# Two adaLN layers on one core: own tiles for the last batch's second layer, and a new order table

## The chip, the core and the metric

The kernel runs on one core of one Trainium2 chip. The metric is the device time of one execution in microseconds (us); a comparison uses the median of several executions. Engines: TensorE (PE) for matrix products, VectorE (DVE), ScalarE (ACT) and GpSimd (POOL) for the rest, SyncE (SP) for issuing transfers. Each engine works off its own list of instructions in order, and waits on semaphores for the others.

## The reference

Eight batches of 512 tokens of width 128 pass through two layers. `adaln` stands for layer norm times (1 + c) plus s, with s and c from a small product of the batch's conditioning row; `g` is a gate row of the same product.

```python
# layer 0, per batch
h = layernorm(x) * (1 + ca) + sa
q, k, v = split(h @ w_qkv.T, heads=16)      # head width 8
q, k = rope(q), rope(k)
x = x + ga * (softmax(q @ k.T) @ v) @ w_out.T
h = layernorm(x) * (1 + cb) + sb
w = softmax over the two largest of h @ gate_kernel
x = x + gb * sum_e w[e] * ((silu(h @ w0[e]) * (h @ w1[e])) @ wo[e])   # 8 experts
# layer 1, per batch
h = layernorm(x) * (1 + ca) + sa            # its own s, c, g
n = layernorm(h) * ln_g + ln_b
v, gate = split(silu(n @ W_hidden + b_hidden))
qk = silu(n @ W_qk + b_qk)
q, k = qk * gamma[0] + beta[0], qk * gamma[1] + beta[1]
a = sum(softmax(q.T @ k / 512), -1)         # one number for each hidden unit
x = x + ga * ((v * a * gate) @ W_out + b_out + h)
h = layernorm(x) * (1 + cb) + sb
x = x + gb * (gelu(h @ w1[batch] + b1[batch]) @ w2[batch] + b2[batch])
```

## The kernel before

A batch goes through four stages. P prepares attention: normalise, transpose, project the query rows (n = 0) and key rows (n = 1), rotate them, and split each into three bfloat16 parts, which go by way of DRAM into the stacked tiles qs and ks; it also makes v. A is attention: a pass over the maxima (scores_for_max, reduced on DVE into negmax), then exponentials on ACT, products with v. B is the layer's experts: POOL scatters the rows of a batch by indirect transfers into slots sorted by expert (xs_d), the expert products run on tiles of slots, and POOL gathers the results (y) back. The last batch runs all eight experts densely instead and has no indirect transfers. C is the second layer.

The order on each engine is written down. The table `SLOTS` gives each step of each batch a place in the list of each engine; `order_of` (L333) sorts it and `walk` (L605) issues it. On all engines steps of several batches are interleaved: while one batch has its exponentials, an earlier one has its experts and a still earlier one its second layer. A wait is written as `after(engine, name, batch, count)`.

Names that the change touches:

- Tiles of stage C: xcn holds the normalised rows (L1799, twice per batch), hc the modulated rows (L705, L707), xdn the rows normalised for the last product, x3 the rows after attention (L2036) and later the result (L2065, L2070), stored by SP (L949, L953). All have one copy. So batch b waits on DVE for x3 of batch b-1 before it writes xcn and hc, and for the store of batch b-1 before it writes x3. nt and nt3 are views of xcn and xdn for the transposed rows. The last batch does the modulation (L705, L707) on DVE and not on POOL, and has banks of its own on PE.
- POOL L2108 takes the power that gives rstd for the last batch; L2112 to L2119 do this for the others; L2200 adds b2 to x3; L2189 and L2191 multiply w2 and b2 by the gate row; L2210 scales the last batch's expert weights.
- PE: L1285 sim, L1311 the output product, L1361 the down product, L1324 the bias pairs that open the up banks of the last batch, L1334 its up product, L1349 its down product, L1005 transposes.
- Stage P of batch 0: L1715, L1720, L1725 split a rotated projection, L1755 to L1759 rotate it (rot1, rot2, rem). Both projections go to bank m1 (shared_pc in the profile), so the second waits until the first is rotated. ACT L1399 rounds W_hidden, L1404 to L1408 copy late constants, L1472 copies v.
- SP: `p_store` (L816) stores three parts of the queries or keys behind one wait for the last part; `p_stack` (L829) loads both stacks behind a wait for all six stores; `mrow_out` (L853) sends a row of maxima; `fetch_weights` (L877) fills the ring of expert weights.

## Time and profile before

| | us |
|---|---|
| median of 3 runs | 979.07 (977.38 to 991.94) |
| the profiled execution | 982.85 |
| its span, first to last instruction | 981.0 |
| PE busy | 831.7 (85%) |
| DVE busy | 696.9 (71%) |
| ACT busy | 579.7 (59%) |
| POOL busy | 461.6 (47%) |

The mean granted clock of PE over the span was 0.916 of full speed. Busy times leave out register, semaphore and transfer-issuing instructions, except for indirect transfers of POOL. A row of the timeline gives the start, the length, the engine, the line of the program, the tiles written and read, and in brackets how long the engine had been idle and what ended that. The releaser "issue" means that the profile shows nothing that the engine waited for, "remote" that it waited for a semaphore whose setter the profile does not show.

### The profile page before, as it was taken

What the parts mean: (1) busy time and instruction counts of PE and PEld (TensorE: products, weight loads), DVE (VectorE), ACT (ScalarE), POOL (GpSimd) and SP (SyncE); (2) the same over time, 40 slices, a digit from 0 to 9 for tenths busy, and PEclk for the clock granted to TensorE, in tenths of its full rate; (3) what the DMA queues carried; (4) which work ended last, traced back from release to release, by engine and by line L of the source; (5) the groups of instructions that cost most, each with busy time, mean ns of one, the idle gap of its engine ahead of it and who ended that gap; (6) DMA issues with size and microseconds to landing.
All of it is one profiled execution on the core that took longest, in us unless ns stands there. A gap on an engine that the chain in (4) does not pass through costs nothing. (4 is left out here: it accounts for less than half of the span.)

```text
span 981.0 us, 15587 instructions
## 1 busy us (share of the span) xinstructions
PE 831.7 (85%) x4972; PEld 449.9 (46%) x4972; DVE 696.9 (71%) x1454; ACT 579.7 (59%) x923; POOL 461.6 (47%) x607
## 2 busy tenths in 40 slices
PE   4788888998789978998899989988899888799586
PEld 3222232544245515654464544634564557376353
DVE  6888786688678756788678658847877435577574
ACT  2256676575567466866686668546857864443252
POOL 0152144025458535573747367383645763663201
PEclk9558889999899979999999989989999999889688
DMA  7524344354824354446073613680156045010001
GB/s 207 164 92 99 73 99 164 86 161 130 208 52 148 122 165 92 113 123 192 25 214 95 202 28 114 182 247 17 42 179 198 25 147 180 24 39 19 1 12 38
DMA packets 97063, 110.77 MB, mean 113 GB/s; under 512 B 14191, under 2 KB 76783, under 8 KB 95616
## 3 DMA queue, kind: packets, MB, share of 16 engines
q1 hardware_dynamic: 92954, 102.06, 36.6%
q0 software_dynamic: 3584, 7.35, 2.6%
q8 instruction: 41, 0.67, 0.3%
q10 hardware_dynamic: 444, 0.36, 0.1%
q14 instruction: 40, 0.33, 0.1%
HBM read 84.06 MB, written 26.26 MB: 112 GB/s over the span
## 5 line engine op out<-in xcount | busy, mean ns | idle before, releaser
L1459 ACT ACTIVATE probs<-scores 128x1024 f32<-128x1024 f32 x256 | 262.0, 1024 | 116.0 <-PE scores L1077 84.8
L1772 DVE TENSOR_REDUCE negmax<-scores_for_max 128x2 f32<-128x1024 f32 x192 | 234.3, 1220 | 59.0 <-PE scores_for_max L1052 45.8
L1087 PE MATMUL weighted_values<-probs,vaug 128*32 128x512 f32 x1024 | 147.6, 653 | 1.1 <-ACT probs L1459 1.1
L1149 PE MATMUL expert_units<-xt,ring 128*128 128x128 f32 x840 | 122.7, 289 | 13.4 <-DVE mu L1949 5.6
L1077 PE MATMUL scores<-qs,ks 51*128 51x512 bf16 x512 | 106.0, 407 | 32.3 <-ACT probs L1459 27.9
L1149 PEld LDWEIGHTS expert_units<-xt,ring 128*128 128x128 f32 x840 | 105.2, 195 | 56.3 <-issue 47.6
L1052 PE MATMUL scores_for_max<-ks,qs 48*128 48x512 bf16 x384 | 76.8, 396 | 15.8 <-DVE negmax L1772 11.3
L2222 POOL DMA_INDIRECT xs_d<-xbn,rowpos x56 | 55.6, 994 | 50.2 <-DVE rowpos L1905 35.4
L2233 POOL DMA_INDIRECT y<-ys_d,rowpos x56 | 55.4, 989 | 37.9 <-DMA ys_d<-slot_rows 21.4
L1077 PEld LDWEIGHTS scores<-qs,ks 51*128 51x128 bf16 x512 | 25.5, 94 | 103.2 <-ACT probs L1459 64.2
L1768 DVE TENSOR_REDUCE negmax<-scores_for_max 128x1 f32<-128x512 f32 x86 | 56.4, 682 | 7.5 <-PE scores_for_max L1046 3.6
L1949 DVE SCALAR_TENSOR_TENSOR mu<-th,expert_units 128x512 f32<-128x512 f32 (+1 forms) x56 | 36.3, 648 | 31.3 <-ACT th L1514 30.2
L1204 PE MATMUL shared_ab<-ring,mu 128*128 128x128 f32 x420 | 54.7, 282 | 3.3 <-DVE mu L1959 2.0
L1204 PEld LDWEIGHTS shared_ab<-ring,mu 128*128 128x128 f32 x420 | 50.2, 194 | 13.1 <-DVE mu L1959 7.2
L2163 POOL CAST mpart<-negmax 128x16 bf16<-128x16 f32 x32 | 6.4, 201 | 102.7 <-DVE negmax L1772 64.3
L1052 PEld LDWEIGHTS scores_for_max<-ks,qs 48*128 48x128 bf16 x384 | 18.7, 94 | 74.1 <-DVE negmax L1772 47.0
L1514 ACT ACTIVATE th<-expert_units 128x512 f32<-128x512 f32 (+1 forms) x56 | 31.9, 570 | 26.0 <-PE expert_units L1149 25.8
L1959 DVE TENSOR_TENSOR mu<-mu,expert_units 128x512 f32<-128x512 f32 (+1 forms) x56 | 36.3, 648 | 15.3 <-PE expert_units L1149 14.3
L1087 PEld LDWEIGHTS weighted_values<-probs,vaug 128*32 128x32 f32 x1024 | 21.0, 111 | 41.2 <-issue 37.7
L1046 PE MATMUL scores_for_max<-ks,qs 48*128 48x512 bf16 x86 | 35.6, 483 | 3.7 <-DVE negmax L1768 3.6
L1339 PE MATMUL shared_pc<-xdn,w 128*128 128x512 f32 x56 | 33.3, 679 | 6.4 <-DVE u L2045 6.0
L1592 ACT ACTIVATE slot_rows<-shared_ab 128x512 f32<-128x512 f32 (+1 forms) x28 | 15.9, 569 | 34.1 <-PE shared_ab L1204 27.3
(325 smaller groups left out, 1666.3 us busy)
## 6 DMA issues: line engine op xcount, KB each, us to landing
ring<-in_experts SPq DMA_DIRECT2D x113, 384.0 KB, 5.2
slot_rows<-xs_d SPq DMA_DIRECT2D x7, 960.0 KB
parts_d<-parts SPq DMA_DIRECT2D x15, 384.0 KB, 2.6
qs<-parts_d SPq DMA_DIRECT2D x14, 384.0 KB
ks<-parts_d SPq DMA_DIRECT2D x14, 384.0 KB
ys_d<-slot_rows SPq DMA_DIRECT2D x21, 256.0 KB
w<-in_L_ffn_w SPq DMA_DIRECT2D x16, 256.0 KB
parts_d<-parts SPq DMA_DIRECT2D x15, 256.0 KB, 2.9
```

Source lines behind the costliest of these rows:

```text
L1052: last = nc.tensor.matmul(sm[:, 512 * m:512 * (m + 1)], qs[at, b % 2, p, t * P:(t + 1) * P], ks[at, b % 2, p, :], start=True, stop=True)
L1077: last = nc.tensor.matmul(se[:, 512 * m:512 * (m + 1)], ks[at, b % 2, p, kt * P:(kt + 1) * P], qs[at, b % 2, p, :], start=True, stop=True)
L1087: last = nc.tensor.matmul(pv[32 * j:32 * j + 32, :], vaug[:, kt, PAIRS * (j // 2) + GP * g + j % 2, :], probs[:, kt % 2, j % 2, j // 2, :] ...
L1149: last = nc.tensor.matmul(dst[:, at], ring[:, q % RING, j, first + f * P:first + (f + 1) * P], xt[:, q % 2, at], start=True, stop=True)
L1204: last = nc.tensor.matmul(m0[:, at], mu[:, (HALVES * q + f) % 4, at], ring[:, q % RING, j, 2 * HID + f * D:2 * HID + (f + 1) * D], start=( ...
L1459: nc.scalar.activation(probs[:, kt % 2, j, :, :].rearrange("p m s -> p (m s)"), se[:, :], ACT.Exp)\
L1768: V.tensor_reduce(negmax[:, g % 2, m, n:n + 1], max_unit_bank(u), AX, ALU.max, negate=True)\
L1772: V.tensor_reduce(negmax[:, g % 2, :, n], sm[:, :].rearrange("p (m s) -> p m s", m=2), AX, ALU.max, negate=True)\
L1949: V.scalar_tensor_tensor(out=mu[:, u % 4, at], in0=th[:, u % 2, at], scalar=1.0, in1=wp[:, at], op0=ALU.add, op1=ALU.mult).then_inc(sig["b ...
L1959: V.tensor_tensor(mu[:, u % 4, at], mu[:, u % 4, at], wp[:, at], ALU.mult).then_inc(sig["b_mu"], 1)
L2222: G.indirect_dma_start(xs_d[:, :], bass.IndirectOffsetOnAxis(ap=rowpos[:, b % 2, c, t:t + 1], axis=0), xbn[:, t, :], None).then_inc(sig["b ...
L2233: G.indirect_dma_start(back[c][:, t, :], None, ys_d[:, :], bass.IndirectOffsetOnAxis(ap=rowpos[:, b % 2, c, t:t + 1], axis=0))\
```

## The change

1. The last batch's second layer has tiles of its own, all free by then: vtok for xcn, xp for hc, x1's first copy for xdn, otok for x3. Its waits for x3, for the result and for the store of batch 6 are gone.
2. In the first batch the key projection goes to bank m0 and its rotation to uz, u2 and nt3, so that it need not wait for the rotation of the query rows. A later use of bank and tiles waits instead (for the last part of the keys). One of the banks of the modulation product moves from m0 to wp, and the wait for its copy from the first transpose of maxima to the third unit of maxima.
3. SP's store of the parts has one slot for each part with a wait for that part alone, and the load of the stacks one for queries and one for keys. The first batch's stacks come in 2 pieces each in place of 4.
4. The table is new for all engines, found by a search in which TensorE's signals are held back inside runs of indirect transfers. Nothing in the code says so; only the numbers differ. The late constants now stand at the head of SP's list.

```diff
-    ("P", "store"): [(n,) for n in range(2)],
+    ("P", "store"): [(n, k) for n in range(2) for k in range(PARTS)],
+    ("P", "stack"): [(n,) for n in range(2)],
...
-        ("B", "fold"): dict(pool=(4, 7, 8, 9, 10, 11, 12, 13, 14, 15, 16, 17, 18, 19, 303, 304)),
+        ("B", "fold"): dict(pool=(2, 4, 5, 6, 7, 8, 10, 11, 12, 13, 14, 15, 16, 17, 303, 321)),
...
+M0_USES["P", "proj"] = ("p_rot", lambda n: n + 1)
...
+        nt_last, nt3_last = (z[:, :, :].rearrange("p t d -> p (t d)") for z in (vtok, x1[:, 0]))
...
-        mod_bank = [[m0[0:NB, 0:3 * D], pv[0:NB, 0:3 * D]], [se[0:NB, 0:3 * D], se[0:NB, 512:512 + 3 * D]]]
+        mod_bank = [[wp[0:NB, 0:3 * D], pv[0:NB, 0:3 * D]], [se[0:NB, 0:3 * D], se[0:NB, 512:512 + 3 * D]]]
...
+        def proj_bank(b, n):
+            return m0 if (b, n) == (0, 1) else m1
+
+        def turned(b, n):
+
+            return (uz, u2, nt3) if (b, n) == (0, 1) else (rot1, rot2, rem)
...
+        def xcn_of(b):
+
+            return vtok if b == LAST else xcn
...
+            return xp if b == LAST else hc
...
+            return x1[:, 0] if b == LAST else xdn
...
+            return otok if b == LAST else x3
...
         def second_modulation(eng, E, b):
             after(eng, "c_in", b, 32 if b == LAST else 16)
             after(eng, "c_xn", b, 1)
-            after(eng, "c_x3", b - 1, 1)
+            if b != LAST:
+                after(eng, "c_x3", b - 1, 1)
...
-            def p_store(b, which):
-
-                after_all(sp, ("p_part2", b, which + 1))
+            def p_store(b, which, k):
+
+                after(sp, f"p_part{k}", b, which + 1)
                 stack_loaded(sp, b - 1)
...
+            def p_stack(b, n):
+
+                after(sp, f"p_stored{n}", b, 16 * PARTS)
+                after(sp, "a_sef", b - 2, 32)
...
                     after(dve, wait, b, 3)
-                    after(dve, *free(b))
+                    if b != LAST:
+                        after(dve, *free(b))
...
             def res(b):
                 after(dve, "c_o", b, 1)
                 after(dve, "c_keep", b, 1)
-                after(dve, "c_stored", b - 1, 16)
+                if b != LAST:
+                    after(dve, "c_stored", b - 1, 16)
```

Where DVE begins the second layer of the last batch, its list before was this (c_ names are stage C; x2 of the last batch, x3 of batch 6):

```order
L1745 TENSOR_SCALAR rstd_c<-mv_c 128x4 [waits c_mv]
L2000 SCALAR_TENSOR_TENSOR qt<-shared_pc,uz 128x512 [waits c_g,c_gk,c_vg,c_hz]
L2005 TENSOR_TENSOR vg<-qz,qt 128x512 [waits c_o,c_hs]
L2036 TENSOR_TENSOR x3<-shared_pc,hc 128x512 [waits c_stored,c_keep,c_o]
L1737 BN_STATS stats_d<-x3 128x6 [waits c_x3]
L1737 BN_STATS stats_d<-x3 128x6 x3
L1741 BN_AGGR mv_d<-stats_d 128x2 [waits c_mv3s]
L1741 BN_AGGR mv_d<-stats_d 128x2 x3
L1799 TENSOR_SCALAR xcn<-x2,mv_c,rstd_c 128x128 [waits c_x3,c_rstd]
L1799 TENSOR_SCALAR xcn<-x2,mv_c,rstd_c 128x128 x3
L705 TENSOR_TENSOR hc<-xcn,crow 128x512 [waits c_x3,c_xn,c_in]
L707 TENSOR_TENSOR hc<-hc,crow 128x512 [waits c_m1]
```

and is now this:

```order
L1783 TENSOR_SCALAR rstd_c<-mv_c 128x4 [waits c_mv]
L2043 SCALAR_TENSOR_TENSOR qt<-shared_pc,uz 128x512 [waits c_g,c_gk,c_vg,c_hz]
L2048 TENSOR_TENSOR vg<-qz,qt 128x512 [waits c_o,c_hs]
L1841 TENSOR_SCALAR vtok<-x2,mv_c,rstd_c 128x128 [waits c_rstd]
L1841 TENSOR_SCALAR vtok<-x2,mv_c,rstd_c 128x128 x3
L741 TENSOR_TENSOR xp<-vtok,crow 128x512 [waits c_xn,c_in]
L743 TENSOR_TENSOR xp<-xp,crow 128x512 [waits c_m1]
L2080 TENSOR_TENSOR x3<-shared_pc,hc 128x512 [waits c_stored,c_keep,c_o]
L1775 BN_STATS stats_c<-xp 128x6 [waits c_h]
L1775 BN_STATS stats_c<-xp 128x6 x3
L1779 BN_AGGR mv_c<-stats_c 128x2 [waits c_mv2s]
L1779 BN_AGGR mv_c<-stats_c 128x2 x3
```

The last batch's normalisation and modulation now stand ahead of x3 of batch 6, and the statistics of batch 6 behind those of the last batch.

On PE, at the end of the last batch's sim (shared_ab), the list before was this, with batch 6's down product to shared_pc:

```order
L1285 MATMUL shared_ab<-ring 128x256 x2
L1361 MATMUL shared_pc<-w2,kq 128x128 [waits c_out,c_w2g,c_gl]
L1361 MATMUL shared_pc<-w2,kq 128x128 x7
L1324 MATMUL scores_for_max<-ones,rem 128x512 [waits c_hz,c_begun,c_inu]
L1324 MATMUL scores_for_max<-ones,rem 128x512 [waits c_hz]
L1311 MATMUL expert_units<-wos,vg 128x128 [waits c_begun,c_wo,c_vg]
L1311 MATMUL expert_units<-wos,vg 128x128 x7
L1324 MATMUL scores<-ones,rem 128x512 [waits c_hz,c_begun,c_inu]
L1324 MATMUL scores<-ones,rem 128x512 [waits c_hz]
L1005 MATMUL weighted_values<-first,xdn 128x128 [waits c_qs,c_xn3]
L1005 MATMUL weighted_values<-first,xdn 128x128 x3
```

and is now this, with batch 6's last up product as its first row:

```order
L1370 MATMUL shared_pc<-xdn,w1 128x512 [waits c_ub]
L1342 MATMUL expert_units<-wos,vg 128x128 [waits c_begun,c_wo,c_vg]
L1342 MATMUL expert_units<-wos,vg 128x128 x7
L1392 MATMUL shared_pc<-w2,kq 128x128 [waits c_ub,c_w2g,c_gl]
L1392 MATMUL shared_pc<-w2,kq 128x128 x7
L1355 MATMUL scores_for_max<-ones,rem 128x512 [waits c_hz,c_begun,c_inu]
L1355 MATMUL scores_for_max<-ones,rem 128x512 [waits c_hz]
L1392 MATMUL shared_pc<-w2,kq 128x128 [waits c_out,c_w2g,c_gl]
L1392 MATMUL shared_pc<-w2,kq 128x128 x7
L1035 MATMUL weighted_values<-first,x1 128x128 [waits c_qs,c_xn3]
L1035 MATMUL weighted_values<-first,x1 128x128 x3
L1355 MATMUL scores<-ones,rem 128x512 [waits c_hz,c_begun,c_inu]
```

Batch 6's two down products moved from inside and behind sim to behind the output product, and the second bias pair behind the transposes.

On POOL, around the gathers of batch 6, the list before was this:

```order
L2210 TENSOR_TENSOR ring<-ring,gb 128x4x256 [waits b_in,b_rows,b_we1]
L2112 TENSOR_SCALAR rstd_d<-mv_d 128x4 [waits c_mv3]
L2114 TENSOR_SCALAR shift_d<-mv_d 128x4
L2117 TENSOR_TENSOR rstd_d<-rstd_d,first 128x4 [waits c_rstd3]
L2119 TENSOR_TENSOR shift_d<-shift_d,rstd_d 128x4 [waits c_rstd3]
L2233 DMA y<-ys_d,rowpos 128x128 [waits b_x2,b_stored] x4
L2200 TENSOR_TENSOR x<-x,b 128x512 [waits c_mv3,c_xn3,c_w2g]
L2233 DMA y<-ys_d,rowpos 128x128 [waits b_x2,b_stored] x4
L685 TENSOR_TENSOR y<-y,pw 128x512 [waits b_in,b_pw,b_back]
```

and is now this:

```order
L2156 TENSOR_SCALAR rstd_d<-mv_d 128x4 [waits c_mv3]
L2158 TENSOR_SCALAR shift_d<-mv_d 128x4
L2161 TENSOR_TENSOR rstd_d<-rstd_d,first 128x4 [waits c_rstd3]
L2163 TENSOR_TENSOR shift_d<-shift_d,rstd_d 128x4 [waits c_rstd3]
L2277 DMA y<-ys_d,rowpos 128x128 [waits b_x2,b_stored] x8
L2254 TENSOR_TENSOR ring<-ring,gb 128x4x256 [waits b_in,b_rows,b_we1]
L2244 TENSOR_TENSOR x<-x,b 128x512 [waits c_mv3,c_xn3,c_w2g]
L703 TENSOR_TENSOR y<-y,pw 128x512 [waits b_in,b_pw,b_back]
```

The scaling of the last batch's second ring moved from ahead of an rstd of the second layer to behind the eight gathers.

## Rows read from the trace of the kernel before

**Rows 1.** Busy us (x instructions) of PE, PEld, DVE, ACT, POOL by stretch; PEclk, DMA share, GB/s
```profile
0.00:60.00 60.00, 37.04 (x99) 14.80 (x99) 46.40 (x111) 17.83 (x33) 14.15 (x25) 0.74 0.59 167
60.00:900.00 840.00, 738.59 (x4655) 398.56 (x4654) 601.80 (x1220) 533.69 (x837) 439.21 (x572) 0.94 0.41 118
900.00:981.00 81.00, 56.11 (x223) 36.53 (x222) 48.74 (x124) 28.15 (x53) 8.19 (x10) 0.79 0.08 21
```

**Rows 2.** Groups, scatters; then sums over ten and seven stretches of indirect transfers
```profile
L2222 POOL DMA_INDIRECT xs_d<-xbn,rowpos x56 | 55.6, 994 | 50.2 <-DVE rowpos L1905 35.4
...
sum 132.90, PE 112.35 PEld 55.42 DVE 93.55 ACT 73.71 POOL 101.93; mean PE 11.23 PEld 5.54 DVE 9.35 ACT 7.37 POOL 10.19
...
sum 52.20, PE 49.34 PEld 25.79 DVE 28.52 ACT 29.44 POOL 40.90; mean PE 7.05 PEld 3.68 DVE 4.07 ACT 4.21 POOL 5.84
```

**Rows 3.** Timeline in two runs of transfers: start, length, engine, line, [idle before, releaser]
```profile
340.55 0.38 PE L1052 MATMUL scores_for_max<-ks,qs 48*128 48x512 bf16 x2
...
345.21 1.23 DVE L1772 TENSOR_REDUCE negmax<-scores_for_max 128x2 f32<-128x1024 f32 x1 [2.52 <-remote]
...
260.45 1.23 DVE L1772 TENSOR_REDUCE negmax<-scores_for_max 128x2 f32<-128x1024 f32 x1 [0.49 <-PE scores_for_max L1052]
```

**Rows 4.** Timeline of POOL at 834 us; busy time by stretch from 840 us
```profile
834.48 2.38 POOL L2210 TENSOR_TENSOR ring<-ring,gb 128x1024 f32<-128x1024 f32 x1 [6.13 <-issue]
...
840.00:860.00 20.00, 14.20 (x27) 5.65 (x28) 9.20 (x12) 10.66 (x20) 15.46 (x17) 0.79 0.10 26
860.00:900.00 40.00, 39.04 (x196) 28.38 (x195) 27.95 (x63) 13.03 (x21) 23.79 (x25) 0.93 0.09 24
```

**Rows 5.** Timeline of the beginning: ACT, PE and DVE
```profile
15.90 0.21 ACT L1404 ACTIVATE bhh<-bh 128x4 f32<-128x4 f32 x1 [0.94 <-DMA bout<-in_L_attn_b_out]
...
19.07 0.77 PE L634 MATMUL shared_pc<-hp_hi,wp_lo 128*128 128x512 f32 x1 [2.35 <-DVE rot L1759]
...
27.44 0.69 DVE L1725 TENSOR_TENSOR vg<-rem,vg 128x512 bf16<-128x512 f32 x1 [0.70 <-ACT vg L1488]
```

**Rows 6.** Timeline, last batch's second layer begins
```profile
914.00 1.02 POOL L2108 TENSOR_TENSOR rstd_c<-rstd_c,first 128x4 f32<-128x4 f32 x1 [20.79 <-DVE rstd_c L1745]
914.69 0.69 DVE L2005 TENSOR_TENSOR vg<-qz,qt 128x512 f32<-128x512 f32 x1
...
918.40 0.69 DVE L2036 TENSOR_TENSOR x<-shared_pc,hc 128x512 f32<-128x512 f32 x1 [3.02 <-PE shared_pc L1311]
...
920.33 1.08 DVE L1799 TENSOR_SCALAR xcn<-x,mv_c,rstd_c 128x128 f32<-128x128 f32 x4
...
925.64 2.05 DVE L1799 TENSOR_SCALAR xcn<-hc,mv_c,rstd_c 128x128 f32<-128x128 f32 x4 [1.12 <-POOL rstd_c L2108]
```

**Rows 7.** Timeline, from sim of the last batch to its up product
```profile
953.49 1.95 PE L1361 MATMUL shared_pc<-w,kq 128*128 128x128 f32 x16
...
955.37 1.98 PE L1324 MATMUL scores_for_max<-ones,rem 1*128 1x512 f32 x4
...
956.39 0.43 SPq L941 DMA_DIRECT2D w<-in_L_ffn_w  x1
...
957.51 2.02 PE L1311 MATMUL expert_units<-wos,vg 128*128 128x128 f32 x16 [0.17 <-issue]
...
959.82 1.26 POOL L2189 TENSOR_TENSOR w<-w,cgb 128x512 f32<-128x512 f32 x1 [32.99 <-DMA w<-in_L_ffn_w]
...
960.66 0.69 DVE L2036 TENSOR_TENSOR x<-expert_units,hc 128x512 f32<-128x512 f32 x1 [2.92 <-DMA out<-x]
...
965.25 1.11 PE L1005 MATMUL weighted_values<-first,xdn 128*128 128x128 f32 x4 [3.81 <-DVE xdn L1799]
...
967.24 3.78 PE L1334 MATMUL scores_for_max<-xdn,w 128*128 128x512 f32 x4 [0.87 <-ACT xdn L1428]
```

**Rows 8.** Waits of SP's queue; DMA issues of the page (KB each, us to landing)
```profile
SPq L858 <- ACT mrow L1451: 134.5, 25, 19.4
...
ring<-in_experts SPq DMA_DIRECT2D x113, 384.0 KB, 5.2
```

481 lines of the change are left out of this document (247 added, 234 removed), and 118 rows, old and new, of the table SLOTS.

## The prediction

> **What bounds the kernel now.** I read the page first, then busy time by stretch, the timeline of the stretches that are not full, and the waits. By stretch [rows 1], TensorE (PE) works 37.0 of the first 60 us, 738.6 of the next 840 and 56.1 of the last 81: it idles 23, 101 and 25 us, together 149. No other engine comes near (VectorE, DVE, 697 us in all), so the middle is bound by PE together with the short chains that feed it, and the two ends by chains in which one thing waits for another. A change of order can only take from the 149 us. The changed program has the same matrix work: what is moved or dropped on PE is not a matmul.
>
> **The middle: the search around indirect transfers.** The 112 indirect transfers go out from GpSimd (POOL), 56 scatters of about 1 us [rows 2] and as many gathers, for each batch but the last. They run in 17 stretches, 185.1 us long. PE is busy 112.35 and 49.34 us of them [rows 2], so it idles 23.4 us, 12.6% of their length. Outside them, between 60 and 900 us, it idles 101 − 23.4 = 78 of 655 us, 11.9%. Had the runs of transfers no cost beyond the usual, they would hold 0.119 × 185.1 = 22 us of idle time: the excess is 1.4 us. Held-back signals are real all the same: at 340.55 us PE starts the second pair of a maximum's matmuls, 0.38 us long, and the reduction that needs them starts at 345.21, 4.3 us after their end, with a releaser that the profile does not see ("remote") [rows 3]. But in another run of transfers the reduction at 260.45 starts after 0.49 us of idle time and with its matmul as the seen releaser [rows 3]. So a search that knows of the effect can gain from about nothing (1.4 us) to all idle time inside the runs (23 us).
>
> A second source is the end of the middle. At 834.48 POOL scales the last batch's second ring of expert weights, after 6.1 us of its queue standing still, and only behind it come an rstd of the second layer and the eight gathers of batch 6 [rows 4]. From 840 to 860 us PE works 14.2 of 20 us and POOL 15.5 [rows 4]. In the new order this scaling stands behind the eight gathers. That frees its 2.4 us of POOL at once, and up to the 5.8 us that PE idles there. Between 860 and 900 PE is full (39.0 of 40, [rows 4]): what it gets earlier it keeps. I take half of it, 2.9 us, and for the search inside the runs the excess of 1.4 us, nearest to what the comparison of shares shows: 4.3 us together, with 0 and 23 + 5.8 as its ends. The choice of half is mine.
>
> **The beginning.** The late constants are now loaded ahead of the rotary tables, and ScalarE (ACT) copies them ahead of v. Before, these copies waited for the last constant until 15.90 us, then took 1.3 us [rows 5]. The load moves ahead by three transfers of some 0.5 us each in SP's queue, and v's copy now waits for that block: about 14.3 + 1.3, so that the first projection starts up to 1.2 us later. Against this the second projection no longer waits for the first's bank: it stood 2.35 us until the last rotation had read it, at 19.07 [rows 5], and can now start behind the first at once. Its three rotations no longer stand between the split's steps, which hides two waits of 0.7 us for ACT and saves 1.5 to 2 us ahead of the last part of the keys, done at 28.13 (27.44 + 0.69) [rows 5]. The sum is a last key part 0.2 to 0.6 us earlier; from there to the first maxima the loads and the second batch's own projection have the same length. First maxima: 0.3 us earlier, bounds −2 and +2. Behind them DVE's maxima follow without a gap, so this 0.3 passes on.
>
> **The last batch's second layer.** Here the edit is plain. POOL's power that gives the rstd of batch 7's x2 ends at 915.02 (914.00 + 1.02); but the normalised rows start at 920.33, since their tile xcn waits for x3 of batch 6, which waits for its output product, on DVE at 918.40 [rows 6]. With vtok in place of xcn only vg of batch 6 stands ahead, until 915.38: 920.33 − 915.4 = 4.9 us earlier. The new order then puts x3 of batch 6 between the modulation (done about 918.1) and the second statistics. It still waits for the product until 918.4, so the statistics start at 919.1, end near 920.7, POOL's power 1.0 later at 921.8, and the second normalisation (1.08 us, as at 920.33) ends at 923.0 in place of 927.69: **4.7 us earlier**. That normalisation took 2.05 us at 925.64 [rows 6], beside POOL's addition of b2, against 1.08 at 920.33. If it does so again beside POOL's rstd of batch 6, only 3.7 us remain. The Trainium skill (SBUF — State Buffer, Who interferes with whom) says that VectorE and GpSimd share one pair of ports as an exclusive lock; by that rule the slower value would hold whenever POOL works at that moment. The rows agree in this pair.
>
> From there the chain of instructions to sim is the same. In sim stood one down product of batch 6, 1.95 us like the one at 953.49 [rows 7]; now up products do, of about 1.1 us (a bias pair's 1.98 halved, and the gaps). So the output product comes 4.7 + 0.9 = 5.6, say 5.7 us earlier: from 957.51 to 951.8. x3 of the last batch waited at 960.66 for batch 6's store, 1.1 us after the product's end (959.53) [rows 7]; that wait is gone: x3 starts near 953.9, 6.8 us earlier, and the normalised rows for the next transpose, 4.6 us behind it, are ready near 958.5.
>
> But PE is not free then. Both down products of batch 6 (1.95 us each) and the first bias pair (1.98) now stand between the output product and that transpose; before, both down products were done earlier. 953.8 + 1.95 + 1.98 + 1.95 = 959.7, with a gap or two 960.2 in place of 965.25 [rows 7]: 5.1 us. The second bias pair (1.98) stands now behind the transpose (1.11). Before, 1.99 us went from the transpose to the first up product at 967.24; now 3.1: 1.1 us lost, 4.0 left. The first four up matmuls took 3.78 us where four of the bias kind take 1.98; PE had idled 3.81 us ahead of the transpose [rows 7]. Now it comes from unbroken work. If half of the 1.8 us comes back, the gain is 4.9. I take **4.5 us**, with 2 (below) and 5.8 as its ends.
>
> What is late next: w2's load cannot start before the second down product has read w, about 959.7. It was 3.4 us on its way (issued 956.39, scaled from 959.82), and scaling takes 1.26 [rows 7]: ready near 965.0, one to two us before the first down product wants it (972.64 − 4.5 less what gelu saves). The cover is thin: with 2 us more on its way the gain at the end falls to about 3.
>
> **The sum.** 982.85 (the profiled execution's own time) − 0.3 − 4.3 − 4.5 = 973.75. The profiled execution lies 3.8 us above the median of the runs shown, 979.07, so the median becomes 969.95, in round figures 970.
>
> **The rivals.**
> First, the search repays in full. For it: waits with no seen releaser inside the runs [rows 3], and that all five engines' orders changed throughout. Against it: PE's idle share inside the runs is that of the rest. 23.4 + 5.8 + 4.8 = 34 taken off: 979.07 − 34 = 945 at the very best, 956 with two thirds of it. Chance 0.18.
>
> Second, the end gives nothing: batch 6's down products, the bias pairs and w2's load fill the time saved. For it: three of them now stand ahead of the last transpose. Against it: the sums above. 970 + 4.5 = 974.5, and if the middle also gives nothing 978.7. Chance 0.22, for both.
>
> Third, slower: the SP queue. It is worked off in order. Its stores of the key and query parts are now six slots with a wait each, and a fetch of the next batch's expert weights or a row of maxima stands between two of them. Already the queue stood longest for ACT, 134.5 us in 25 waits with one of 19.4, and a fetch takes 5.2 us to land [rows 8]. The order shows such a place in batches 3, 4 and 6. Where a fetch goes out later than the rings come free, the expert products of that batch start late by up to one landing: three times 5.2 = 15.6, and 970 + 15.6 = 986; with the middle's 4.3 lost as well, 990. It decides from the point where a fetch's slack (the rings it fills are free that much before their products are due) is smaller than the wait for one part; such waits in this queue are 5.4 us on average (134.5 / 25). Against it: parts are ready early where they were stored together before. Chance 0.12, of which 0.06 is beyond 2%.
>
> Fourth, the middle is only shuffled: gains and losses of 2 to 4 us in the batches cancel, the ends give their 4.8. 974.3. This is the lower end of my own case and belongs to it.
>
> **How the numbers follow.** My case (965 to 978) has 0.48, the full search 0.18, nothing at the end 0.22, slower 0.12. Two per cent of 979.07 is 19.6 us, about what a measurement of this kernel can tell from no change: below 959.5 is faster, above 998.7 slower. Only the first rival reaches beyond the first bound, with a small tail of my case: 0.18. Beyond the second only mishaps larger than the third rival's price: 0.06. The rest, 0.76, is within. The range for 8 in 10 goes from 955 (most of the first rival) to 984 (half of the third).
>
> **What would show it.** Right: batch 7's first normalisation starts within half a us of its power on POOL, and x3 of batch 7 right at the end of the output product; the last transpose starts at once behind batch 6's second down product; the time from the power's end at 915.02 to the end of the span falls from 66.0 (981.0 − 915.0) to 61.5 us; PE's idle time from 60 to 900 us falls from 101 to 97. Wrong: if that idle time falls by more than 10, the search was worth more than the shares say; if it grows, look at waits of the rings for their fetch and at PE's waits for weights. If POOL's scaling of w2 ends after the last gelu, w2 is the next bound. If the first maximum starts after 38.2 us, the copies of constants ahead of v cost more than the second bank gives.

## The result: slower by 0.6%, and where 6.7 us went

The changed kernel takes 990.07 us (median of 19 runs, 982.24 to 998.65); the kernel before, run beside it, 983.32 us (19 runs, 977.38 to 991.94). The ratio is 1.0064, with a 95% interval from 1.0041 to 1.0087: slower by some 6 us, where 9 us less had been forecast. Both lie within 2% of each other. The profiled execution took 993.16 us, its span 991.4 (before 981.0).

The experiments below were run on four chips. On two of them the kernel before takes 981 to 983 us, on the other two 961 to 962; they are called the first and the second kind here. For the result above, and the trace of before, no chip is on record; by their times and their waits they are of the first kind. Each ratio below is to the kernel before, run beside it on the same chip. Ratios and intervals leave out the few executions that fell in a slower state of the chip, and a ratio can differ by up to 0.25% from the quotient of the two medians.

The page of the changed kernel, busy time over the whole span, and then its busy time by stretch (us, instructions, granted clock, DMA share, GB/s):

```profile
PE 829.2 (84%) x4972; PEld 453.5 (46%) x4972; DVE 696.9 (70%) x1454; ACT 578.5 (58%) x923; POOL 459.7 (46%) x607
```

```profile
0.00:60.00 60.00, 31.39 (x83) 14.45 (x83) 44.50 (x107) 16.16 (x32) 13.90 (x26) 0.76 0.63 170
60.00:840.00 780.00, 680.99 (x4388) 363.46 (x4389) 559.56 (x1136) 506.09 (x791) 392.70 (x528) 0.93 0.44 120
840.00:860.00 20.00, 18.19 (x79) 10.71 (x79) 10.18 (x19) 8.56 (x14) 8.40 (x10) 1.00 0.58 190
860.00:900.00 40.00, 28.45 (x132) 18.81 (x132) 26.63 (x54) 16.46 (x30) 28.91 (x29) 0.83 0.12 32
900.00:991.00 91.00, 70.23 (x292) 46.09 (x290) 56.03 (x140) 31.21 (x57) 15.78 (x17) 0.86 0.08 19
```

The busy time of every engine is what it was before, to 3 us. PE's idle time is what grew: in the first 60 us 28.6 in place of 23.0, from 60 to 900 us 112.4 in place of 101.4 [rows 1], and only behind 900 us it fell, 20.8 in place of 24.9.

**The end** gave nearly what was forecast. The timeline of the last batch's second layer:

```profile
927.97 1.02 POOL L2152 TENSOR_TENSOR rstd_c<-rstd_c,first 128x4 f32<-128x4 f32 x1 [16.02 <-DVE rstd_c L1783]
...
929.26 1.11 DVE L1841 TENSOR_SCALAR vtok<-x,mv_c,rstd_c 128x128 f32<-128x128 f32 x4
...
936.64 1.08 DVE L1841 TENSOR_SCALAR vtok<-xp,mv_c,rstd_c 128x128 f32<-128x128 f32 x4
...
966.10 3.62 PE L1342 MATMUL expert_units<-wos,vg 128*128 128x128 f32 x16 [2.55 <-issue]
...
969.76 0.69 DVE L2080 TENSOR_TENSOR otok<-expert_units,xp 128x512 f32<-128x512 f32 x1 [1.77 <-PE expert_units L1342]
...
975.24 0.60 PE L1035 MATMUL weighted_values<-first,x 128*128 128x128 f32 x4
...
977.68 1.98 PE L1365 MATMUL scores_for_max<-x,w 128*128 128x512 f32 x4
...
980.19 1.28 POOL L2233 TENSOR_TENSOR w<-w,cgb 128x512 f32<-128x512 f32 x1 [7.04 <-DMA w<-in_L_ffn_w]
```

The first normalisation starts 0.3 us behind its power (before 5.3, [rows 6]). From the end of that power, 928.99, to the end of the span it is 62.4 us; before it was 981.0 − 915.0 = 66.0. So the last layer is 3.6 us shorter. Everything else lies ahead of it: that power ends 14.0 us later than before.

**The beginning** lost 6.5 us. The timeline of ACT, PE and DVE, first of the changed kernel with one rotation, the sixteenth maximum and the first exponentials, then the last two of the kernel before:

```profile
16.76 0.76 PE L645 MATMUL shared_pc<-hp_hi,wp_lo 128*128 128x512 f32 x1 [2.55 <-ACT vtok L1504]
...
18.18 0.63 PE L645 MATMUL shared_ab<-hp_hi,wp_lo 128*128 128x512 f32 x1
...
26.82 0.69 DVE L1759 TENSOR_TENSOR vg<-xdn,vg 128x512 bf16<-128x512 f32 x1 [0.70 <-ACT vg L1520]
...
42.55 0.69 DVE L1795 TENSOR_TENSOR rot<-shared_pc,cosT 128x512 f32<-128x512 f32 x1 [0.57 <-PE shared_pc L647]
...
53.51 0.68 DVE L1808 TENSOR_REDUCE negmax<-scores_for_max 128x1 f32<-128x512 f32 x1
...
60.69 1.02 ACT L1491 ACTIVATE probs<-scores 128x1024 f32<-128x1024 f32 x1 [0.97 <-PE scores L1108]
```

```profile
47.15 0.68 DVE L1768 TENSOR_REDUCE negmax<-scores_for_max 128x1 f32<-128x512 f32 x1
...
54.19 1.02 ACT L1459 ACTIVATE probs<-scores 128x1024 f32<-128x1024 f32 x1 [0.33 <-PE scores L1077]
```

The last key part is ready at 27.51, 0.6 us earlier than the 28.13 of [rows 5], as forecast, and the first maximum starts at the same 38.1 us in both. But the first sixteen maxima of batch 0 go together through POOL, PE, ACT and a transfer ahead of the first exponentials. DVE's new list has four rotation steps like the one at 42.55 and a later batch's statistics between them, the old one nothing, and DVE also waits for PE more often. The sixteenth starts at 53.51 in place of 47.15, 6.4 us later.

**Behind 60 us** the waits are the place to look. A summary of waits lists each instruction's idle time by releaser (us in total, times, longest). The longest and the most telling rows of before whose releaser is not seen, then those of after:

```profile
ACT probs L1459 <- remote: 10.1, 4, 5.0
...
DVE negmax L1772 <- remote: 5.4, 2, 2.9
```

```profile
DVE negmax L1812 <- remote: 19.1, 7, 5.8
ACT probs L1491 <- remote: 12.8, 4, 4.8
ACT mrow L1483 <- remote: 8.0, 1, 8.0
```

With the rows left out it is 38.3 us in 14 waits before, and 66.0 in 20 after. By the timelines every one of these 34 waits is of ACT or DVE and ends in a run of POOL's indirect transfers or at most 1.8 us behind it. Each is for a semaphore that only PE sets, and the semaphore's update comes 1.6 to 6.0 us behind the end of PE's instruction: the signal itself is late. POOL issues 112 of these transfers in both kernels, 143.0 us in 27 runs before and 142.2 us in 21 runs after (a run ends where 1.6 us pass without one). PE idles 16.8 us inside the runs before and 27.3 after, outside them 84.6 and 85.1. So the table that was searched with held-back signals has longer runs and more held-back waits, and nearly all of the growth of PE's idle time from 60 to 900 us lies inside the runs. How much of it the held-back signals make is another question, which the plain transfers below answer in part. The clearest place is batch 0's eight scatters, L2266, back to back:

```profile
151.97 1.21 POOL L2266 DMA_INDIRECT xs_d<-xbn,rowpos  x1 [4.42 <-DVE rowpos L1948]
...
158.83 0.39 PE L1108 MATMUL scores<-qs,ks 51*128 51x512 bf16 x2 [0.64 <-issue]
...
161.07 0.96 POOL L2266 DMA_INDIRECT xs_d<-xbn,rowpos  x1 [0.30 <-issue]
...
162.90 0.22 POOL L2213 TENSOR_TENSOR mpart<-mrem,mpart 128x16 bf16<-128x16 f32 x1
...
163.60 1.02 ACT L1491 ACTIVATE probs<-scores 128x1024 f32<-128x1024 f32 x1 [4.82 <-remote]
163.62 1.23 DVE L1812 TENSOR_REDUCE negmax<-scores_for_max 128x2 f32<-128x1024 f32 x1 [5.85 <-remote]
...
164.68 0.60 PE L1108 MATMUL scores<-qs,ks 51*128 51x512 bf16 x2 [5.46 <-ACT probs L1491]
```

PE's product for the exponentials ends at 159.22, and ACT reads it at 163.60, 4.4 us later, together with DVE. POOL's mpart, for which this negmax waits too, ended only at 163.12: most of the 5.85 us of this wait would be there with no signal held back, so the 66.0 us are more than what held-back signals make engines wait. Then PE works at its lower level for 20 us more. Busy time and granted clock (the number behind POOL) in steps of 5 us:

```profile
160.00:165.00 5.00, 0.32 (x2) 0.11 (x2) 1.38 (x2) 1.02 (x1) 3.80 (x7) 0.55 0.91 304
165.00:170.00 5.00, 4.66 (x21) 0.83 (x23) 2.61 (x4) 3.27 (x5) 0.50 (x1) 0.50 0.77 232
...
180.00:185.00 5.00, 4.96 (x24) 2.58 (x23) 2.17 (x3) 4.07 (x6) 2.31 (x2) 0.56 0.36 121
185.00:190.00 5.00, 5.00 (x41) 2.67 (x37) 3.38 (x4) 2.51 (x3) 0.83 (x4) 1.00 0.11 37
```

0.50 is 1.2 of 2.4 GHz. Ahead of the fall PE had stood still from 159.22 to 164.68. At this level the two matmuls of L1108 take 0.60 us in place of 0.39.

A second place is 866 us, where the scaling of the last batch's ring moved behind the gathers:

```profile
864.75 2.36 POOL L2254 TENSOR_TENSOR ring<-ring,gb 128x1024 f32<-128x1024 f32 x1
...
866.67 4.19 DVE L2101 SCALAR_TENSOR_TENSOR kq<-u,uz 128x512 f32<-128x512 f32 x1 [0.70 <-ACT u L1632]
867.05 1.27 POOL L2244 TENSOR_TENSOR x<-x,b 128x512 f32<-128x512 f32 x1
...
872.97 2.07 PE L1370 MATMUL shared_pc<-xdn,w 128*128 128x512 f32 x2 [4.88 <-DVE u L2089]
```

DVE's L2101 takes some 0.69 us in most of its 28 places and 4.19 here, beside four POOL operations without a gap between them, and PE waits 4.88 us for the chain behind it. Before, the same step took 1.31 us. The Trainium skill (SBUF — State Buffer, Who interferes with whom) says that a DVE instruction with two inputs in SBUF contends with a GpSimd instruction that reads SBUF, for ports that only one of them can hold. This row agrees. From 840 to 860 us PE's idle time fell from 5.8 us [rows 4] to 1.8, and from 860 to 900 it rose from 1.0 to 11.6; but the changed kernel is some 12 us late by then, so these stretches hold other work. Nearly the same work is compared from the first gather of batch 6 to the end of the power, first before, then after:

```profile
841.90:915.02 73.12, 64.47 (x271) 41.22 (x269) 45.92 (x104) 28.88 (x52) 39.02 (x39) 0.89 0.10 27
```

```profile
854.45:928.99 74.54, 60.01 (x266) 38.01 (x264) 48.03 (x103) 27.97 (x51) 41.78 (x40) 0.91 0.11 29
```

PE idles 14.5 us in place of 8.7, but is busy 4.5 us less, and the stretch is only 1.4 us longer. The other 12.6 of the 14.0 us were lost ahead of these gathers.

### The profile page after: what moved, and what is told of

Same layout as the page of the kernel before. It is cut to its first block, busy times and chain, and to the rows that moved or that the text cites. A ratio compares the mean times of both kernels' runs of the same rounds, so it can differ in the third digit from the quotient of the medians.

```text
span 991.4 us, 15608 instructions
## 1 busy us (share of the span) xinstructions
PE 829.2 (84%) x4972; PEld 453.5 (46%) x4972; DVE 696.9 (70%) x1454; ACT 578.5 (58%) x923; POOL 459.7 (46%) x607
## 4 chain that ended last, share of the span: by engine, by line
PE 48%; DVE 18%; ACT 15%; issue 10%; another core or an unknown queue 4%; POOL 3%; SPq 1%; DMA 1%; DVEq 0%; ACTq 0%; POOLq 0%
PE weighted_values L1118 8%; PE expert_units L1180 7%; PE scores L1108 6%; ACT probs L1491 5%; DVE negmax L1812 5%; PE shared_ab L1235 4%; PE scores_for_max L1084 3%; PE shared_pc L1392 3%; PE shared_pc L1316 2%; PE shared_pc L1342 2%; PE scores L1187 1%; DVE mu L1992 1%; DVE kq L2101 1%; PE shared_pc L1370 1%
## 5 line engine op out<-in xcount | busy, mean ns | idle before, releaser
L1108 PE MATMUL scores<-qs,ks 51*128 51x512 bf16 x512 | 106.6, 411 | 28.9 <-ACT probs L1491 25.9
L1180 PEld LDWEIGHTS expert_units<-xt,ring 128*128 128x128 f32 x840 | 107.4, 198 | 45.1 <-issue 42.4
L1084 PE MATMUL scores_for_max<-ks,qs 48*128 48x512 bf16 x384 | 78.6, 405 | 22.5 <-DVE negmax L1812 18.0
L2266 POOL DMA_INDIRECT xs_d<-xbn,rowpos x56 | 55.2, 986 | 47.2 <-DVE rowpos L1948 32.0
L2277 POOL DMA_INDIRECT y<-ys_d,rowpos x56 | 54.6, 974 | 38.3 <-DMA ys_d<-slot_rows 21.5
L1108 PEld LDWEIGHTS scores<-qs,ks 51*128 51x128 bf16 x512 | 25.6, 94 | 94.7 <-ACT probs L1491 60.5
L1235 PE MATMUL shared_ab<-ring,mu 128*128 128x128 f32 x420 | 57.7, 285 | 5.1 <-DVE mu L2002 3.4
L1235 PEld LDWEIGHTS shared_ab<-ring,mu 128*128 128x128 f32 x420 | 51.7, 195 | 16.4 <-issue 11.6
L1992 DVE SCALAR_TENSOR_TENSOR mu<-th,expert_units 128x512 f32<-128x512 f32 (+1 forms) x56 | 36.3, 647 | 20.7 <-ACT th L1546 15.5
L1118 PEld LDWEIGHTS weighted_values<-probs,vaug 128*32 128x32 f32 x1024 | 21.4, 112 | 41.8 <-issue 37.3
L1078 PE MATMUL scores_for_max<-ks,qs 48*128 48x512 bf16 x86 | 31.6, 448 | 9.8 <-DVE negmax L1808 6.6
L2089 DVE SCALAR_TENSOR_TENSOR u<-shared_pc,uz 128x512 f32<-128x512 f32 x28 | 19.2, 687 | 26.9 <-ACT shared_pc L1602 26.5
```

The lines of the kernel that those rows point to most:

```text
L1084: last = nc.tensor.matmul(sm[:, 512 * m:512 * (m + 1)], qs[at, b % 2, p, t * P:(t + 1) * P], ks[at, b % 2, p, :], start=True, stop=True)
L1108: last = nc.tensor.matmul(se[:, 512 * m:512 * (m + 1)], ks[at, b % 2, p, kt * P:(kt + 1) * P], qs[at, b % 2, p, :], start=True, stop=True)
L1118: last = nc.tensor.matmul(pv[32 * j:32 * j + 32, :], vaug[:, kt, PAIRS * (j // 2) + GP * g + j % 2, :], probs[:, kt % 2, j % 2, j // 2, :] ...
L1180: last = nc.tensor.matmul(dst[:, at], ring[:, q % RING, j, first + f * P:first + (f + 1) * P], xt[:, q % 2, at], start=True, stop=True)
L1235: last = nc.tensor.matmul(m0[:, at], mu[:, (HALVES * q + f) % 4, at], ring[:, q % RING, j, 2 * HID + f * D:2 * HID + (f + 1) * D], start=( ...
L1992: V.scalar_tensor_tensor(out=mu[:, u % 4, at], in0=th[:, u % 2, at], scalar=1.0, in1=wp[:, at], op0=ALU.add, op1=ALU.mult).then_inc(sig["b ...
```

## The experiments

### Which part of the change: code, end, beginning, middle

All of these are built from the two tables: the list of each engine follows one table up to a cut and the other behind it. Cut lines: first maxima (38 us), first exponentials done with batch 0's maxima (some 95 us), 300 us, and the begin of the last batch's second layer. The first four ran side by side on one chip of the first kind. e1 has the new code for the end's tiles and SP's split, but not the second bank, and before's order; e2 adds the new order behind the last cut.

Of e1 against the changed kernel, and behind it a row of e2's table against e1's:

```diff
         def proj_bank(b, n):
-            return m0 if (b, n) == (0, 1) else m1
+            return m1
```

```diff
-        ("C", "res"): dict(dve=(526, 612, 694, 784, 854, 900, 952, 979)),
+        ("C", "res"): dict(dve=(526, 612, 694, 784, 854, 900, 954, 977)),
```

> The changed kernel's tiles for the last batch and its split stores, but the order table of the kernel before (each old store slot becomes three in a row), and without the second bank and tiles in the first batch. Theory A (all of the loss is the new order): as before, 983 us, less about 1 us for the store wait that is gone, ratio 0.998 to 1.000. Rival B (the split stores hold up SP's queue by themselves): 3 us or more above before.

984.42 us, ratio 1.0010 (0.9973 to 1.0048).

> As e1, but from the last batch's second layer on the order of the changed kernel. If the edit at the end is worth what the two traces show (66.0 us from the power to the end before, 62.5 after): 3.5 to 4.5 us below before, 979 us, ratio 0.996. Rival: the end of the changed kernel only looks short because the work ahead of it was late, then 0 to 1 us below before.

979.28 us, ratio 0.9965 (0.9930 to 1.0001). The code alone costs nothing that can be measured, SP's six slots among it, as long as they stand together. The end's order is worth 0.45% against e1, 4.4 us; the intervals overlap, but the profiles agree: from the end of the last batch's first power to the end of the span it is 67.4 us in e1 and 62.1 in e2.

e3 has all new code and the new order to 95 us, before's behind it; e4 before's order to 95 us and the new one behind it.

A row of e3's table against e1's:

```diff
-        ("P", "stats"): dict(dve=(120, 197, 287, 346, 398, 462, 540, 647)),
+        ("P", "stats"): dict(dve=(120, 239, 282, 346, 398, 462, 540, 647)),
```

> The changed kernel with its own order up to the end of the first batch's attention, and the order of before from there. Theory A1 (the start is made up for later, the middle is the cause): 983 us, within 1.5 of before. Rival A2 (the first exponentials come 6.5 us later and nothing takes it back): 988 to 989 us, ratio 1.006.

993.38 us, ratio 1.0105 (1.0068 to 1.0143).

> The start of before (order, one bank, one set of tiles), and from the end of the first batch's attention on the order of the changed kernel, its end too. Theory A1: the loss of the middle stays, 987 to 991 us. Rival A2 (the start is the cause): 983.3 less the 4 us of the end, 979 to 984 us.

988.98 us, ratio 1.0062 (1.0024 to 1.0101). It holds the gain of the end, so its middle alone loses about 10 us against e2. Both beginning and middle lose, and not in sum: in the changed kernel the two together cost less than the sum of each.

e7 (second kind) takes the new order to the first maxima only.

> The changed kernel's start only up to its first units of maxima (order of the loads, copies ahead of v, second bank), the order of before from there. Theory S1 (the copies of late constants ahead of v and the later normalisation of the second batch are what costs): 6 to 10 us above before, as with the whole new start. Rival S2 (the cost comes from rotations placed between the first maxima): within 2 us of before.

959.88 us, ratio 0.9983 (0.9958 to 1.0007): loads, copies and the second bank cost nothing, as the prediction had it. The next four ran side by side on one chip of the first kind. e8 is e7 with the new end. e11 goes with the new order to 95 us, e9 from 38 us to 95 us like before and then like the new table to 300 us, e10 like the new table from 300 us; all have the new end.

POOL's places of the scatters of batches 0 and 1 in e9 against e8, of batches 2 and 3 in e10 against e8, and the second and third batch's statistics in e11 against e8:

```diff
-        ("B", "scatter"): dict(pool=(51, 53, 54, 55, 56, 57, 59, 60, 77, 78, 79, 81, 82, 84, 85, 86,
+        ("B", "scatter"): dict(pool=(52, 53, 54, 55, 56, 57, 58, 59, 80, 81, 82, 83, 84, 86, 87, 88,
```

```diff
-        119, 120, 121, 122, 123, 124, 125, 126, 150, 154, 155, 157, 159, 160, 161, 162,
+        117, 118, 119, 120, 121, 122, 123, 124, 156, 158, 160, 161, 163, 164, 165, 166,
```

```diff
-        ("P", "stats"): dict(dve=(120, 239, 287, 346, 398, 462, 540, 647)),
+        ("P", "stats"): dict(dve=(120, 239, 282, 346, 398, 462, 540, 647)),
```

> The best of the pieces so far: the changed kernel's code, its order up to the first maxima and from the last batch's second layer on, and the order of before for all that lies between. Theory P (the pieces add up: 0.9983 for the load, 0.9965 for the end): ratio 0.995, 4 to 6 us below before. Rival (each piece's gain is taken back when the other moves): 0.998 to 1.000.

976.47 us, ratio 0.9976 (0.9942 to 1.0010).

> As e8, but with the changed kernel's order through the first batch's attention too, where rotations of the next batches stand between its maxima. Theory S2 (this interleaving costs what e3 lost): 8 to 12 us above e8. Rival (e3's 10 us were a matter of that chip or of its few executions): within 3 us of e8.

983.42 us, ratio 1.0011 (0.9978 to 1.0044): by the ratios 0.35% above e8, 3.4 us for the interleaved maxima (7.0 by the medians), but the intervals overlap, so this is not sure. e3's loss of 1.05% with the same beginning isn't seen again; what parts the two stays open.

> As e8, but with the changed kernel's order from the end of the first batch's attention to the fourth batch's first maxima, some 95 to 300 us. Theory P with the middle's 10 us spread evenly: a quarter to a third, 2 to 4 us above e8. If the loss has one place and that is here: 8 to 10 us above e8.

992.28 us, ratio 1.0106 (1.0060 to 1.0153), 1.3% above e8. Busy time on the pages of e8, then of e9:

```profile
PE 823.0 (84%) x4972; PEld 445.0 (46%) x4972; DVE 694.6 (71%) x1454; ACT 579.6 (59%) x923; POOL 460.6 (47%) x607
```

```profile
PE 842.2 (85%) x4972; PEld 454.4 (46%) x4972; DVE 695.4 (70%) x1454; ACT 578.2 (58%) x923; POOL 459.5 (46%) x607
```

PE's idle time is nearly the same (154.1 and 152.8 us); the 19 us are in busy time, the same matmuls at the lower level. The granted clock from 60 to 300 us is 0.85 in e9 and 0.91 in e8; over the whole span and all their executions the medians are 0.911 and 0.923. So the stretch from 95 to 300 us costs most, and by the clock. It is the one in which batch 0's eight scatters became one row, but everything else in it was moved too. More held-back waits are not what parts the two: those with an unseen releaser are 41.8 us in e9 and 43.1 in e8.

> As e8, but with the changed kernel's order from some 300 us on. Spread evenly: 6 to 8 us above e8. If its one place is the stretch before 300 us: within 2 us of e8.

983.56 us, ratio 1.0025 (0.9991 to 1.0058): the rest of the middle costs 0.5% against e8, with intervals that overlap, and its share is not cut further.

### Are indirect transfers the cause?

The same number of transfers of the same size, but to fixed rows. Left out is the sorting by expert, so the products run on other rows, in the same number.

```diff
-                G.indirect_dma_start(xs_d[:, :], bass.IndirectOffsetOnAxis(ap=rowpos[:, b % 2, c, t:t + 1], axis=0),
-                                     xbn[:, t, :], None).then_inc(sig["b_sent"], 16)
+                G.dma_start(xs_d[(4 * c + t) * P:(4 * c + t + 1) * P, :], xbn[:, t, :]).then_inc(sig["b_sent"], 16)
```

and the gathers likewise. e5 is the kernel before with this edit, e6 the changed one (both second kind), e16 and e17 are the same two on a chip of the first kind.

> The kernel before with plain transfers of the same size from POOL's queue, to and from fixed rows, in place of the 112 indirect ones (so the rows are not sorted by expert, and that part of the result is left out). Theory H (indirect transfers hold back TensorE's signals, some 38 us of waits with no seen releaser): these waits go, and the time falls by 5 to 17 us, to 966 to 978. Rival (POOL is merely busy during them and no one waits for that): within 3 us of before, and the waits with no seen releaser stay.

945.04 us, ratio 0.9819 (0.9786 to 0.9853).

> The same edit in the changed kernel. Theory H with the new table hit harder (PE idles 27.3 us inside the runs of transfers against 16.8): it gains about 10 us more than the kernel before does, so that both are equal less the 4 us of the end. Rival M (the new order of the middle is the worse one whatever the transfers do): the difference of 7 us between the two kernels stays as it is.

949.18 us, ratio 0.9843 (0.9811 to 0.9874).

> The kernel before with plain transfers in place of the 112 indirect ones (rows not sorted by expert), as e5. If the chip is one that holds signals back and indirect transfers are the cause: ratio to before 0.96 to 0.97, that is 10 to 20 us more than the 17 us that e5 gained, and no waits with no seen releaser. If the held signals have another cause: 0.98 and the waits stay. On a chip without them: 0.982 as e5.

949.25 us, ratio 0.9663 (0.9637 to 0.9688), before 982.73.

> The changed kernel with the same edit, as e6. If held signals carry the difference between chips: equal to e16 or up to 4 us from it, on either chip. If the new order loses on this chip for another reason: 6 us or more above e16.

951.34 us, ratio 0.9651 (0.9606 to 0.9695). Without indirect transfers the two kernels are equal (the intervals overlap on both kinds), and the two kinds of chip are nearly so, 945 to 951 us. Indirect transfers cost the kernel before 33.5 us on the first kind and 16.7 on the second. None of the four traces has a wait with an unseen releaser. From the groups of instructions of e5 (busy us, mean ns; e16 has the same to 1 ns), transfers that took 994 ns (scatters, [rows 2]) and 989 ns (gathers):

```profile
L2222 POOL DMA_DIRECT2D xs_d<-xbn x56 | 31.1, 560 | 35.9 <-DVE rowpos L1905 34.8 <-issue 1.1
L2232 POOL DMA_DIRECT2D y<-ys_d x56 | 30.6, 553 | 33.9 <-DMA ys_d<-slot_rows 32.1 <-issue 1.8
```

POOL is less busy too, 409.7 us in e16 and 411.0 in e5, in place of 461.6. That part may be the 16.7 us of the second kind; these runs don't part it from the rest.

These traces also show that the new order idles more by itself. From 60 us to the end of the last batch's first power PE idles 104.2 us before and 115.0 after. With plain transfers it is 84.3 and 92.3 (e5, e6), 82.6 and 91.7 (e16, e17): 8 to 9 us more in the new order with no signal held back at all. There PE is 9.4 and 5.5 us less busy in the whole span, the same matmuls at a higher clock, and this pays for the idle time; with indirect transfers on the first kind it is only 2.5 us less busy. So what the indirect transfers take from the new order shows mostly in PE's busy time. These are single executions.

### The changed kernel where no signal is held back

e12 is the changed kernel itself on a chip of the second kind, so it has no diff. e13 moves one step of POOL: the last maxima part of batch 1 ahead of the fifth scatter of batch 0, which breaks the row of eight. e14 makes batch 0's scatters plain in the changed kernel. e15 does the opposite in the kernel before: it makes batch 0's scatters one row, with the steps that stood between ahead of it and behind it.

The first numbers of the two rows that change in e13 (and in e18 below):

```diff
-        ("A", "mparts"): dict(pool=(30, 37, 41, 44, 45, 46, 48, 60,
+        ("A", "mparts"): dict(pool=(30, 37, 41, 44, 45, 46, 48, 56,
...
-        ("B", "scatter"): dict(pool=(52, 53, 54, 55, 56, 57, 58, 59,
+        ("B", "scatter"): dict(pool=(52, 53, 54, 55, 57, 58, 59, 60,
```

In e14, and in e15 against the kernel before:

```diff
+                if b == 0:
+                    G.dma_start(xs_d[(4 * c + t) * P:(4 * c + t + 1) * P, :], xbn[:, t, :]).then_inc(sig["b_sent"], 16)
+                    return
```

```diff
-        ("B", "scatter"): dict(pool=(51, 53, 54, 55, 56, 57, 59, 60,
+        ("B", "scatter"): dict(pool=(52, 53, 54, 55, 56, 57, 58, 59,
```

> The changed kernel as it is, with its order table written out once more, as the reference for the three runs beside it: ratio to before 1.004 to 1.009.

958.53 us beside 960.97 for the kernel before: ratio 0.9957 (0.9929 to 0.9986). The same kernel that loses 0.6% on the first kind gains 0.4% here. Its trace has no wait with an unseen releaser; PE idles 98.1 us from 60 to 900. The timeline at batch 0's row of scatters:

```profile
158.71 0.38 PE L982 MATMUL scores<-qs,ks 51*128 51x512 bf16 x2
159.13 1.02 ACT L1365 ACTIVATE probs<-scores 128x1024 f32<-128x1024 f32 x1 [0.51 <-PE scores L982]
...
162.15 1.02 ACT L1365 ACTIVATE probs<-scores 128x1024 f32<-128x1024 f32 x1 [0.49 <-PE scores L982]
...
163.58 0.22 POOL L2087 TENSOR_TENSOR mpart<-mrem,mpart 128x16 bf16<-128x16 f32 x1
...
163.83 1.23 DVE L1686 TENSOR_REDUCE negmax<-scores_for_max 128x2 f32<-128x1024 f32 x1 [5.38 <-POOL mpart L2087]
```

Here ACT goes on during the row: its exponentials start within 0.1 us of the product's end, not 4.4 us behind it. DVE's maxima stand 5.38 us all the same, and for a seen reason: POOL's mpart stands behind all eight scatters. In the old order it stands behind them too, but there DVE had other work, and its maximum at 157.86 waited 0.44 us for it. So two things met in that row on the first kind: a real wait of DVE, and a held signal for ACT.

> The changed kernel with one step of POOL moved: the fourth parts of the second batch's maxima stand between the first four and the last four scatters of the first batch, not behind all eight. Theory R (the unbroken row holds PE's signals until its end at 162 us, PE idles 5 us and its clock stays low for 24 us): 5 to 12 us below e12. Rival O (the row is incidental, the order around it costs): within 3 us of e12.

957.07 us, ratio 0.9971 (0.9936 to 1.0006): no gain over e12, although DVE's wait for mpart is gone.

> The changed kernel with the first batch's eight scatters as plain transfers to fixed rows (that batch's rows are then not sorted by expert; all other transfers are indirect as before). Theory R: 8 to 12 us below e12, and no waits with no seen releaser between 152 and 165 us. Rival O: within 3 us of e12.

955.76 us, ratio 0.9915 (0.9881 to 0.9949), 0.4% less than e12; the intervals overlap.

> The kernel before with POOL's order changed in one place only: the first batch's eight scatters in one row, with the two steps that stood between them put ahead and behind. Theory R: 4 to 10 us above before. Rival O: within 2 us of before.

963.69 us, ratio 1.0025 (0.9996 to 1.0055): on this kind the row costs the kernel before nothing that is sure.

e18 is e13 on a chip of the first kind.

> The changed kernel with the first batch's row of scatters broken in two by the step that stood behind it, as e13. On a chip with held signals, if the unbroken row is a main part of the loss: 5 us or more below the changed kernel, ratio to before 1.001 or less. If one row more or less does not matter: 1.004 to 1.008. On a chip without: 0.997 as e13.

979.48 us, ratio 0.9977 (0.9952 to 1.0001), against 1.0064 (1.0041 to 1.0087) of the changed kernel in its own comparison on this kind; the intervals are apart. As far as two comparisons on different chips can tell, one step moved takes the whole loss away, where on the second kind it does nothing. Its timeline in the broken row, and its busy time on the page:

```profile
158.44 0.22 POOL L2087 TENSOR_TENSOR mpart<-mrem,mpart 128x16 bf16<-128x16 f32 x1
...
158.70 1.23 DVE L1686 TENSOR_REDUCE negmax<-scores_for_max 128x2 f32<-128x1024 f32 x1 [0.68 <-POOL mpart L2087]
159.15 1.01 POOL L2140 DMA_INDIRECT xs_d<-xbn,rowpos  x1 [0.49 <-issue]
...
160.20 1.02 ACT L1365 ACTIVATE probs<-scores 128x1024 f32<-128x1024 f32 x1 [0.49 <-issue]
```

```profile
PE 813.7 (83%) x4972; PEld 451.0 (46%) x4972; DVE 697.8 (71%) x1454; ACT 578.1 (59%) x923; POOL 460.4 (47%) x607
```

The held-back wait at this place is gone, and in all 44.0 us of them in 17 waits remain, in place of 66.0. PE's idle time from 60 to 900 us is the same as in the changed kernel (112.3 and 112.4 us). The span is 14.9 us shorter because PE is 15.5 us less busy: the same matmuls at a higher granted clock, 0.929 in place of 0.911 (medians over all executions 0.927 and 0.916). Most of this does not lie where the step was moved: from 60 to 300 us the clock is 0.91 in place of 0.89, from 300 to 900 us 0.97 in place of 0.94. How one step at 157 us does this is not shown.

## Why the prediction was wrong

**The end: right.** Forecast 4.5 us off; the profile gives 3.6 (62.4 for 66.0; 61.5 was forecast), e2 against e1 4.4. Counted from the power's end, the output product starts 37.1 us behind it (forecast 36.8), x3 of the last batch 40.8 (38.9), since the product, at a granted clock of 0.57 from 966 to 970 us, took 3.6 us in place of 2.0; the transpose 46.2 (45.2). The first four up matmuls took 1.98 in place of 3.78, but this gave nothing: from there to the end it is 13.7 us, before 13.8. Without it the sum stood at 4.0; I took 4.5, and 3.6 came. The cover of w2 was as thin as said: POOL ends at 981.47, and PE's first down product starts at 981.76, for DVE. x3 of the last batch starts at once with its product's end, as forecast. The second normalisation took 1.08 us at 936.64 although small POOL operations (128x4) ran beside it, so "whenever POOL works" was too wide.

**The beginning: right to 38 us, wrong behind it.** e7 bears out the small sum. But "Behind them DVE's maxima follow without a gap, so this 0.3 passes on" failed: I took it from the old list. In the new list steps of other batches stand between the maxima, the sixteenth comes 6.4 us later, and the first exponentials start 6.5 us later; e11 against e8 leaves 3.4 us of it in the time, not surely.

**The middle: wrong in size and in sign**, and this decides. The term was a gain of 4.3 us, 1.4 for the search and 2.9 for the ring. Measured, the new middle costs: e4 against e2, both with the new end and the old beginning, is about 10 us slower, with intervals apart. I set the worth of held-back signals by comparing idle shares inside and outside the runs of transfers in the old order: an excess of 1.4 us. The total of the 14 unseen waits, 38.3 us, was in the same trace and I did not put it into the sum. With plain transfers before's time falls by 33.5 us on this kind and by 16.7 us on the other: if held signals are what parts the kinds, they are worth about 17 us, 12 times my term. A normal idle share inside the runs did not show that they cost nothing, and the share leaves out what the clock costs behind a gap. I also gave the search only a gain or nothing; no bound was on the side of a loss. The new table has fewer and longer runs, 66.0 us of unseen waits and 10.5 us more idle time inside them. But 8 to 9 us more idle time come with the new order even with plain transfers, and I had put nothing in the sum for an order that idles more by itself, nor for the clock, which is where e9 and e8 differ.

**The ring at 834 us: wrong.** "Between 860 and 900 PE is full: what it gets earlier it keeps" failed. The scaling didn't vanish from the path but landed beside DVE's kq of batch 5. For nearly the same work (from the first gather of batch 6 to the power's end) PE idles 14.5 us in place of 8.7, and the stretch is 1.4 us longer, where I had taken 2.9 us off. It is the same pair of engines that I had weighed for the second normalisation, where it did not happen: that took 1.08 us at 936.64.

**The base.** 979.07 us was the median of 3 runs; that of 19 is 983.32. So 970 stood 13 us, not 9, below what the kernel before takes, and the upper end of 984 was about no change. The 0.76 for a result within 2% came true, with the sign wrong.

**The rivals.** The third, SP's queue: e1 (1.0010) shows only that six slots together cost nothing, since it has no fetch between them. Against the rival itself speaks the trace of the changed kernel: PE's only waits for a transfer are 3.1 us for ks at 37.5 us and 1.3 us for a row of maxima at 60.0 us, none for a ring. Its outcome, 986 to 990 us, was nearest to the measured one for a reason that is not seen. The second, nothing at the end, falls with 62.4 in place of 66.0 us. The first, a search that repays in full, is refuted on the first kind; even on the second the whole change gives only 0.4%. The fourth, a middle that is only shuffled, 4.8 us off, comes closest to the second kind, where the ratio of e12 is worth 4.1 us.

**What stays open.** The parts do not add up: beginning, 95 to 300 us and the rest cost 0.35, 1.3 and 0.5% one by one, 2.1% together, less 0.45% for the end, but the whole costs 0.64%. Nor does the time follow the unseen waits: e10 has 36.6 us of them at 983.56 us, e9 41.8 at 992.28, e4 63.5 at 988.98. That the clock's falls move with each cut would fit this, but is not shown. The runs do not show why some chips hold signals back, nor on the first kind what PE's granted clock would be without. e18 and the changed kernel were not run on the same chip.

## What to carry to other kernels

Add up the waits whose releaser the profile does not see before you price what causes them: the total shows how large the effect can be, though not what it costs. An idle share that looks normal does not show that they cost nothing. When steps are moved together into one row on an engine, look in the new order for what now stands behind the row, and who waits for it. And where a stall is followed by a lower clock, price the stall with the matmuls behind it, not with its own length.

## What was not expected of the hardware

- ACT and DVE see PE's signals late while POOL issues indirect transfers, on two of the four chips: 37 to 66 us of such waits in a run, the longest 8.0 us, the signals 1.6 to 6.0 us late in the traces before and after. The traces from the other two chips have none, and those with plain transfers of the same size have none.
- The kernel before differs by 2.2% between these chips (983 and 961 us), and with plain transfers by 0.4% (949 and 945): most of the difference hangs on indirect transfers.
- After a gap of 5.5 us without work, PE stood at its lower level for 20 us although it was busy for 4.3 to 5.0 of each 5 us.
- A DVE instruction with two inputs took 4.19 us in place of 0.69 beside a row of four POOL instructions; in e12, on the second kind, the same instruction again took 4.19 us.
